# An unread product behind each score product of the first two attention tiles

## What is computed

```python
x = x + _L0_attn_ref(_layernorm(x, axis=-1), ...)
# inside, b = 8, h = 16 heads, t = 512, d = 16
xq = xq * c + rot_half(xq) * s
xk = xk * c + rot_half(xk) * s
scores = jnp.einsum('bhqd,bhkd->bhqk', xq, xk) / np.sqrt(d)
p = jax.nn.softmax(scores, axis=-1)
o = jnp.einsum('bhqk,bhkd->bhqd', p, xv)
return o @ wo.T + bo
```

## Time and profile before

| | us |
|---|---|
| three runs | 2090.35, 2087.06, 2080.31 |
| their median | 2087.06 |
| the profiled execution | 2072.48 |
| its span | 2070.7 |

### The profile page before, as it was taken

How to read it: one execution, slowest core, us unless ns; L and a number is a source line. 1 busy time by engine, 2 the same in 40 slices (tenths; PEclk the granted TensorE clock), 3 DMA queues, 4 the chain that set the end, 5 groups by cost and what they waited for, 6 DMA issues and landing times.

```text
span 2070.7 us, 38109 instructions
## 1 busy us (share of the span) xinstructions
PE 1883.1 (91%) x12664; PEld 1367.4 (66%) x12664; DVE 1628.1 (79%) x2246; ACT 1298.1 (63%) x2749; POOL 1357.3 (66%) x1205
## 2 busy tenths in 40 slices
PE   3699999999996999996798989898989898999998
PEld 2344444444445899994577777777777777888776
DVE  4588888898855745653799999999999999976664
ACT  3167766677762433343787878787878777844443
POOL 4344445544344344442799999999999999966665
PEclk8599999999998999998899999999999999999999
DMA  5766666656326354562514040405050507001100
GB/s 106 121 102 112 110 107 118 120 100 131 79 87 214 74 103 73 105 135 72 174 28 157 23 162 23 153 20 166 13 173 11 165 11 266 11 32 33 40 30 22
DMA packets 248489, 195.83 MB, mean 95 GB/s; under 512 B 163907, under 2 KB 216923, under 8 KB 247788
## 3 DMA queue, kind: packets, MB, share of 16 engines
q1 hardware_dynamic: 222570, 164.45, 31.0%
q0 software_dynamic: 13296, 17.77, 5.0%
q10 hardware_dynamic: 12434, 11.18, 1.9%
HBM read 138.22 MB, written 55.19 MB: 93 GB/s over the span
## 4 chain that ended last, share of the span: by engine, by line
PE 21%; DVE 20%; issue 7%; ACT 4%; POOL 1%; DVEq 0%; POOLq 0%; ACTq 0%
DVE mb_da_ps L2558 10%; PE mb_da_ps L2016 9%; DVE mb_hp L2554 3%; PE mb_f_ps L2694 3%; DVE mb_hc L2565 3%; PE mb_y_ps L2646 2%; DVE mb_hp L2556 2%; PE mb_f_ps L2690 1%; PE mb_da_ps L2632 1%; PE mb_f_ps L2705 1%; ACT mb_da_ps L2384 1%; DVE mb_f_ps L2610 1%; DVE mb_u L2541 1%; ACT mb_u L2449 1%; PE mb_f_ps L1980 1%
## 5 line engine op out<-in xcount | busy, mean ns | idle before, releaser
L2323 POOL TENSOR_TENSOR mb_dbu<-mb_dtu,mb_bbc 128x1024 f32<-128x1024 f32 x191 | 453.1, 2380 | 51.5 <-DVE mb_hp L2556 32.7
L550 ACT ACTIVATE ex_plain<-at_t_ps 128x512 f32<-128x512 f32 x512 | 290.0, 596 | 170.4 <-PE at_t_ps L983 165.5
L706 DVE TENSOR_REDUCE at_mx<-at_s_ps 128x2 f32<-128x1024 f32 x256 | 311.0, 1219 | 35.1 <-PE at_s_ps L992 31.9
L2329 POOL TENSOR_TENSOR mb_hp<-mb_hp,mb_cbc 128x1024 f32<-128x1024 f32 x128 | 304.9, 2382 | 10.5 <-DVE mb_hp L2554 10.5
L2558 DVE TENSOR_TENSOR_SCAN mb_da_ps<-mb_da_ps,mb_dbu 128x1024 f32<-128x1024 f32 x128 | 292.0, 2281 | 7.1 <-ACT mb_da_ps L2384 6.8
L992 PE MATMUL at_s_ps<-ex_w 48*128 48x512 f32 x512 | 225.8, 498 | 16.2 <-DVE at_mx L706 14.2
L983 PE MATMUL at_t_ps<-ex_w 64*128 64x512 f32 x512 | 220.3, 479 | 10.4 <-ACT ex_plain L550 4.8
L1405 POOL DMA_INDIRECT x<-m_o,m_xs x71 | 113.1, 1593 | 162.1 <-DMA x<-m_o,m_xs 92.6
L983 PEld LDWEIGHTS at_t_ps<-ex_w 64*128 64x128 f32 x512 | 86.1, 189 | 176.7 <-ACT ex_plain L550 138.7
L2646 PE MATMUL mb_y_ps<-lw_ident,mb_hc 128*128 128x128 f32 x1024 | 138.5, 279 | 56.9 <-DVE mb_hc L2565 56.9
L2646 PEld LDWEIGHTS mb_y_ps<-lw_ident,mb_hc 128*128 128x128 f32 x1024 | 115.2, 143 | 89.1 <-DVE mb_hc L2565 74.0
(11 more groups left out here) (388 smaller groups left out, 4684.7 us busy)
## 6 DMA issues: line engine op xcount, KB each, us to landing
mb_cbc<-mb_scr SPq DMA_DIRECT2D x64, 512.0 KB, 6.9
mb_bbc<-mb_scr SPq DMA_DIRECT2D x47, 512.0 KB, 7.3
ex_w<-at_scr SPq DMA_DIRECT2D x126, 128.0 KB, 3.7
m_xs<-rt_rows SPq DMA_DIRECT2D x71, 129.0 KB
at_scr<-at_qk_hi SPq DMA_DIRECT2D x32, 256.0 KB
mb_bbc<-mb_dgs SPq DMA_DIRECT2D x16, 512.0 KB, 7.8
ex_w<-at_scr SPq DMA_DIRECT2D x126, 64.0 KB, 3.7
at_scr<-at_qk_lo SPq DMA_DIRECT2D x28, 256.0 KB
```

Of the source, the lines that this page charges most:

```text
L550: act.activation(probs[:, c, h, :], t_ps[:, k % 2, :], ACT.Exp, scale=SCALE).then_inc(exp_done, 1)
L706: dve.tensor_reduce(out, s_ps[:, m % 2, :, :], AX.X, ALU.max).then_inc(max_done, 1)
L2323: pool.tensor_tensor(dbu[:, q % 3, :, :], dtu_2, bbc[:, 2 * p:2 * p + 2, :], ALU.mult).then_inc(S["dbu_ready"], 1)
L2329: pool.tensor_tensor(hp[:, r, :, :], hp[:, r, :, :], cbc[:, 2 * p:2 * p + 2, :], ALU.mult).then_inc(S["hp_ready"], 1)
```

## The change

`keep_busy` gets the bank as an argument, and in slots -2 and -1 each step issues one unread product into the output bank behind its score product: 32 in all.

```diff
-            def keep_busy(count):
+            def keep_busy(count, bank=score_bank(1)):
 
                 for _ in range(count):
-                    pe.matmul(score_bank(1)[:, 0:D], ident[:, :], wv[:, 0, :], start=True, stop=True)
+                    pe.matmul(bank[:, 0:D], ident[:, :], wv[:, 0, :], start=True, stop=True)
...
                     if (u := tile(t + 2)) is not None:
                         scores(u, k // 2, 1 - k % 2)
+                    if t in (-2, -1):
+                        keep_busy(1, o_ps)
                     if k == 2 and (u := tile(t - 1)) is not None:
                         values(u, 3)
```

## The result

The changed kernel takes 2092.67 us in the median of 10 executions (2085.27 to 2112.96), the kernel before 2085.14 us (2073.04 to 2090.37). The ratio is 1.0059, 95% interval 1.0033 to 1.0085: slower, by about 12 us by this ratio and by 7.5 us between the two medians. When it was timed again beside the experiments the ratio was 1.0038 (1.0013 to 1.0063), about 8 us. The profiled execution is the slowest of the ten, 2112.96 us with a span of 2111.2, so that its profile shows more of the loss than a usual execution has.

What follows compares the result with a forecast made beforehand. Slots -2 and -1 were taken as bound by VectorE, shared-bank blocks and once DMA, not score products. Adding 13.2 (slot -2) + 5.4 (slot -1) - 1.3 (slot 0) = + 17.3 us to the 2087.06 median gave 2104 us, range 2090 to 2114.

Steps and rivals of the forecast that it cites:

- the likeliest case: The forecast itself: slots -2 and -1 lengthen, slot 0 gives a little back; 2104 us, own range 2098 to 2110, chance 0.60.
- the clock rises early: Rival: unread products raise the clock early in slot -2, some 3.5 us after starting; + 8.2 us, 2095 us; chance 0.16.
- A step costs 1.87 us at half and 1.05 us at full clock: Slots -2 and -1: score product plus unread product, priced from alternating rows at the attention stage's end.
- VectorE will wait, the DMA wait ahead of slot -1 disappears, TensorE's queue carries the loss to slot 0: Slots -2 and -1: VectorE waits for TensorE, 2.03 us of DMA wait are used up, slot 0 begins 18.6 us late.
- The clock rises one step behind the query block of slot -2: Clock stays at 0.50 until then; slot -1 starts 13.2 us late, then takes 5.4 us more at full clock.
- Slot 0 gives back 1.3 of 2.5 us: Slot 0 holds a half-clock stretch; if the clock stays up, up to 2.5 us return, half taken: 1.3 us.
- The sum: Slot -2's delay, slot -1's addition and slot 0's return: 13.2 + 5.4 - 1.3 = + 17.3 us.
- The delay is carried to the end: Behind slot 0 TensorE has almost no waits to take up the delay; longest groups 6.2 and 3.7 us.
- Hidden: Rival: in slots -2 and -1 unread products are hidden, steps 0.71 us full, 1.35 half clock; - 2.3 us, 2085; chance 0.10.
- The clock falls again in slot -1: Rival: 16 steps of slot -1 cost 0.82 us more each, + 13 us, 2117 us; chance 0.07.
- Taken up later: Rival: TensorE's small waits in later stages absorb the delay, 2087 us; chance 0.04.

Runs made afterwards that it cites:

- the third profile: The changed kernel run again without edit, for a third profile: execution 2094.1 us; its landmark of slot 1 (start of the turned maxima on TensorE) at 128.7 us.
- the narrow products: Changed kernel with its 32 unread products in the same places, but of 64 columns in place of 256: ratio 1.0096 to the kernel before.
- those of the same kind: Changed kernel with each unread product repeating the score product ahead of it (48 rows, same half of the array): ratio 1.0014 to the kernel before.
- the burst: Changed kernel with eight more unread products in one run at the end of slot -3: ratio 1.0089 to the kernel before.

## Why the prediction came out as it did

Forecast 2104 us within 2090 to 2114, + 17.3 us; measured 2092.67, about + 12 us by the first ratio and + 8 by the second. The direction is right and the time lies within the full range, but outside the 2098 to 2110 that the likeliest case had for itself. It is nearest to the 2095 of "the clock rises early", which occurred in none of the four profiles: in all of them the clock rose at the block where the forecast had it, or a slot later. That the number is inside the range is therefore in part luck.

*A step costs 1.87 us at half and 1.05 us at full clock.* Right to 0.02 us in every profile. The rows from the stage's end, behind a product of 64 rows, hold for one of 48. That much of the cost is in the broken pair and the switch of kind, and not in the columns, was an argument from two rows; two behind the pair, the narrow products and those of the same kind show it. (By the narrow products the 256 columns are 0.72 us of the 1.88, four thirds of 0.54.)

*VectorE will wait, the DMA wait ahead of slot -1 disappears, TensorE's queue carries the loss to slot 0.* Right.

*The clock rises one step behind the query block of slot -2.* Right in one of four profiles, where slot -2 takes 27.99 us (forecast 29.3) and slot -1 19.73 (20.1):

```profile
64.48:92.47 27.99, 27.99 (x122) 13.57 (x121) 11.59 (x15) 0.50 (x2) 7.27 (x18) 0.66 0.57 86
92.47:112.20 19.73, 19.73 (x122) 10.04 (x121) 11.85 (x15) 0.77 (x3) 4.66 (x11) 1.00 0.44 75
```

In the other three it rose a whole slot later. I had allowed one block, 3.3 us; the price of the later rise is 16 us at the landmark (144.6 against 128.7), which my own range did not have. This is the weakest step of the prediction. Its witness for the low clock, the stretch from 612.41 us, was a thin one: up to 620.61 us it holds only two steps of the alternation, with products with the values between them, and at 597 us the same steps ran at 1.00. In the first profile TensorE is marked busy for all of 35.02 us in slot -2, at 0.50 throughout. The rule of the Trainium skill on which the rival "the clock rises early" rested (page "TensorE: Matmul & The Clock Gate", section "Why this matters for your kernels"), that a TensorE kept busy gets its full clock, does not hold of this work, and the measurement decides.

*Slot 0 gives back 1.3 of 2.5 us.* Too little. From slot 0's landmark to slot 1's it is 14.35 us in the third profile and 14.4 in the first, against 17.15: 2.8 us, all of it (2.1 to 2.2 against the other two profiles of the kernel before, where it is 16.6 and 16.5).

*The sum.* At slot 1's landmark the third profile has + 12.7 us where the sum had + 17.3. The 4.6 us apart are the earlier start of slot -2 (0.6), slots -2 and -1 (1.3 and 0.4), the first steps of slot 0 (112.20 to 114.31, 2.1 in place of 3.0), and the 1.5 us given back on top. The other profiles have + 28.7. So the sum lies between the two cases that occurred and is neither.

*The delay is carried to the end.* Not shown. Two of the three executions with the long front are among the longest (2113 us), but the third took 2095.9. And the time rose by about 12 us by the one ratio and 8 by the other, where every profile of the front has + 12.7 or more. The later stages differ from one execution to the next by as much: behind the first Mamba outputs 1117.8 to 1130.8 us in the changed kernel, and 1128.9 in the run with two products behind each pair, whose front is as short as before. Nor does the front alone order the other runs: with the burst it is 4.4 us longer and the ratio 1.0089. The mean granted clock of the twelve shortest executions of the changed kernel, 0.948 to 0.952, is above that of the kernel before, whose timed executions at 2083 to 2088 us mostly have 0.939 to 0.943; so part of the loss in front may be returned as full clock, in the front itself or behind it. Whether the change shifts how often the later stages fall long or short is not settled by one profile of each run; it stays open.

*The rivals.* "The clock rises early" did not occur in the four profiles of the changed kernel, but did with two products behind each pair. "Hidden" is out for this order of products; two behind each pair come out as it says in time, though with steps of another kind. "The clock falls again in slot -1" did not occur in those four profiles, but did with narrow products. "Taken up later" is neither shown nor excluded.

## What to carry over

An unread product is free only where it fits the engine's idle time as the engine really runs it: here it was put inside a pair of products that ran side by side, at the price of a full-array product and two switches of kind, 1.05 us a step at full clock and 1.88 at half, where the slots could bear 0.76. Put it behind the pair, and compare the step with the wait that it is to fill. And a stretch that an engine spends busy at half clock is priced from rows at half clock, with the rise taken as a range over the blocks at which it may come, and not as one of them.

## What the runs showed of the hardware that was not expected

TensorE alternating a 48-row product with a full-array float32 one was marked busy without a break for 35 us and kept the granted clock 0.50 (1.2 GHz). With two full-array products in a row behind each pair the clock rose at 69.2 us, before the query block, in the one profile taken. With the same instructions the clock rose within the same query block in one execution (at 83.4 us) and only at the next slot's block in three (at 119.4 to 119.6 us). With a quarter of the unread columns the kernel was slower than with all of them (1.0096 against 1.0059 and 1.0038), and its one profile spent all of slot -1 at half clock. And the clock of the front was of no consequence to the kernel before: 95.4 to 96.2 us to slot 0 with a clock that was up for a part of slots -2 and -1 or for none.
